# Second layer norm's rows in a buffer of their own, low-rank sums in the ring of back banks, and a new order of work

## What is computed

```python
x = x + tanh(g_xattn[0]) * cross_attention(layernorm(x), ctx)      # q with rotary positions, k and v of 128 context rows, 8 heads
x = x + tanh(g_ffn[0])   * ffn0(layernorm(x))
x = x + tanh(g_xattn[1]) * (layernorm(x) @ W1.T + mean_part(ctx) + b)
x = x + tanh(g_ffn[1])   * ffn1(x_normed)                           # x_normed = layernorm(x)

# ffn0, with ternary weights (values -1, 0, 1 times a scale of the row)
h = x @ Wfc.T + gate * (x @ v.T @ fast_b.T @ u.T)                   # 2048 hidden numbers, rank 16
out = relu(h)**2 @ Wproj.T

# ffn1, with ternary weights and rows rounded to integers of at most 127
h = gelu(rint(127 * n(x) / max|n(x)|) ... @ w1.T + b1)              # n: RMS norm
out = rint(127 * n(h) / max|n(h)|) ... @ w2.T + b2
```

## Time and profile before

| | busy us | share of the span | instructions |
|---|---|---|---|
| PE | 1094.3 | 93% | 8270 |
| DVE | 953.5 | 81% | 1989 |
| ACT | 799.4 | 68% | 1575 |
| POOL | 591.5 | 50% | 567 |

### The profile page before, as it was taken

How to read it: one execution, slowest core, us unless ns; L and a number is a source line. 1 busy time by engine, 2 the same in 40 slices (tenths; PEclk the granted TensorE clock), 3 DMA queues, 4 the chain that set the end, 5 groups by cost and what they waited for, 6 DMA issues and landing times.

```text
span 1176.7 us, 22172 instructions
## 1 busy us (share of the span) xinstructions
PE 1094.3 (93%) x8270; PEld 677.4 (58%) x8558; DVE 953.5 (81%) x1989; ACT 799.4 (68%) x1575; POOL 591.5 (50%) x567
## 2 busy tenths in 40 slices
PE   5776699999999999999899999999999999999997
PEld 5544456474655656475655656475656656564654
DVE  4796868778789888788878798898879886998667
ACT  3988947676683958576584857676674957586545
POOL 4243545464653746454544656555545555564431
PEclk9888799999999999999999999999999999999999
DMA  9959651434525343533625252443436242432210
GB/s 339 367 153 309 204 122 47 99 81 77 126 59 117 69 116 73 104 81 68 126 53 136 57 123 68 89 110 77 108 55 145 45 119 61 103 69 55 68 45 27
DMA packets 273802, 128.11 MB, mean 109 GB/s; under 512 B 247568, under 2 KB 248080, under 8 KB 272016
## 3 DMA queue, kind: packets, MB, share of 16 engines
q1 hardware_dynamic: 273136, 125.73, 41.8%
q10 hardware_dynamic: 560, 0.96, 0.3%
HBM read 57.19 MB, written 8.39 MB: 56 GB/s over the span
## 4 chain that ended last, share of the span: by engine, by line
PE 55%; ACT 17%; DVE 16%; POOL 5%; issue 4%; DMA 2%; SPq 0%; ACTq 0%; DVEq 0%
PE ps L1861 14%; PE ps L1835 10%; PE ps L1904 6%; PE ps L1920 5%; PE ps L1788 5%; ACT e L966 4%; PE ps L1735 4%; PE ps L1883 4%; ACT rl L1002 3%; ACT hid L1007 2%; ACT sq L1013 2%; PE ps L1760 1%; DVE st L1369 1%; PE ps L1841 1%; PE ps L1775 1%
## 5 line engine op out<-in xcount | busy, mean ns | idle before, releaser
L1835 PE MATMUL ps<-xT,fcT 128*128 128x256 f16 x2048 | 262.5, 276 | 10.8 <-ACT rl L1002 7.1
L749 POOL TENSOR_TENSOR rs<-ve,nhalf 128x1 f32<-128x1 f32 x160 | 101.7, 638 | 306.1 <-DVE ve L1374 222.8
L1861 PE MATMUL ps<-pjT,hid 128*128 128x512 fp8e4 x1024 | 232.3, 379 | 2.6 <-POOL hid L776 1.6
L1835 PEld LDWEIGHTS ps<-xT,fcT 128*128 128x128 fp8e4 x2048 | 200.1, 99 | 52.6 <-ACT rl L1002 10.0
L776 POOL TENSOR_TENSOR hid<-sq,hid 128x512 f16<-128x512 f32 x128 | 163.1, 1279 | 80.3 <-ACT sq L1013 79.4
L1861 PEld LDWEIGHTS ps<-pjT,hid 128*128 128x128 f16 x1024 | 98.0, 98 | 98.3
L1002 ACT ACTIVATE rl<-ps,rsf 128x256 f32<-128x256 f32 x256 | 106.4, 469 | 25.0 <-PE ps L1841 24.8
L966 ACT ACTIVATE e<-ps,nmb,sig 128x128 f32<-128x128 f32 x256 | 113.1, 462 | 7.2 <-DVE nmb L1412 6.9
L1904 PE MATMUL ps<-w1T,q4T 128*128 128x512 fp8e4 x480 | 114.2, 379 | 0.7 <-issue 0.6
L1058 ACT ACTIVATE q<-h 128x2048 f16<-128x2048 f32 x30 | 57.3, 1910 | 79.3 <-DVE h L1531 79.3
L781 POOL TENSOR_TENSOR e<-e,einv 128x512 f32<-128x512 f32 x64 | 70.1, 1100 | 78.5 <-DVE einv L1416 78.5
(11 more groups left out here) (243 smaller groups left out, 2025.7 us busy)
## 6 DMA issues: line engine op xcount, KB each, us to landing
xb<-in_x SPq DMA_DIRECT2D x16, 512.0 KB, 3.6
xa<-in_x SPq DMA_DIRECT2D x15, 512.0 KB, 4.0
out<-r SPq DMA_DIRECT2D x30, 256.0 KB, 2.3
rope<-in_rope SPq DMA_DIRECT2D x16, 384.0 KB, 3.2
h<-in_w1T SPq DMA_DIRECT2D x6, 1024.0 KB, 5.8
h<-in_w2T SPq DMA_DIRECT2D x6, 1024.0 KB, 6.4
h<-in_wkvT SPq DMA_DIRECT2D x2, 1024.0 KB, 12.6
hid<-in_w_fc SPq DMA_DIRECT2D x2, 1024.0 KB, 9.9
```

Source lines behind the costliest of these rows:

```text
L1835: pe.matmul(ps[:, FFN0 + m % 2, a * G:(a + 1) * G], fcT[:, k, f * P:(f + 1) * P], xT2[:, xs, k, :], start=(xs == 0 and k == 0), stop=False)
L1861: mm = pe.matmul(ps[:, FFN0 + t, :], hid[:, xs, c, t * P:(t + 1) * P], pjT[:, c, :], start=(c == 0 and xs == 0), stop=(c == FC - 1 and xs ...
```

## The change

1. `xn2` gets its own buffer of 128 x 2 x 512 numbers. `ln2_apply(g)` now waits for `x2lo` of group g-1, its own earlier reader. To make room, constants and small rows of the prologue (`ones`, `small`, `wsum`, `fold1`, `bnd`, `gsf`, `bxbc`, `tb2`) share buffers with things that are used later or earlier.
2. The low-rank rows and sums of group g go, from group 2 on, to the ring of back banks: the ring has 14 slots for a group, and slot 11 of group g-2 is theirs, columns 0 to 255 for the rows, 256 to 511 for the sum. w2's slots move by one. `low_rows(g)` waits for `h_done` of group g-2 in place of group g-1's down product. `up` of m=1 waits for the down product of g-1, and the scores of g > 2 wait for `low_r(g-1)`. The first w1 piece of the last group but one waits for the low-rank remainder of the last.
3. The softmax takes banks 2 and 3 together: three maxima and three scalings for each group in place of four and four.
4. The MAGIC subtraction for ffn1's input rows moves from DVE (L1509, 30 instructions) to ACT, as a copy with a bias in a function `q4_integers`, with a semaphore `q4_int`; `ln3_apply` waits for it of group g-1.
5. All number tables are new. Up to about 105 us the order of every engine's work is as before.

In all PE has the same number of instructions, DVE 62 fewer, ACT 30 more, POOL and SP as many as before.

```diff
-        xn2 = rl
+        xn2 = sb("xn2", [P, TILES, D], F32)
...
+        def s_pair():
+            return slice(ROW_TILES[2], ROW_TILES[3] + 1)
...
-            return ps[:, BACK0 + (13 * g + slot) % 3, :]
+            return ps[:, BACK0 + (14 * g + slot) % 3, :]
+
+        def low_bank(g):
+            return ps[:, FFN0 + 1, :] if g < 2 else back_bank(g - 2, 11)
...
             PE=dict(
-                low_sum=((34,), (62,), (97,), (134,), (175,), (214,), (253,), (291,), (332,), (371,), (411,),
+                low_sum=((34,), (62,), (99,), (136,), (177,), (215,), (253,), (291,), (332,), (372,), (411,),
...
-                need(sp, q4_done, 2 * TILES, g, 2 * t + 1)
+                need(sp, q4_int, TILES, g, t)
...
-                act.activation(lowsum[:, :], ps[:, FFN0 + 1, 0:G], ACT.Copy).then_inc(part_b, 1)
+                act.activation(lowsum[:, :], low_bank(g)[:, 0:G], ACT.Copy).then_inc(part_b, 1)
...
-                act.activation(tlow[:, :], ps[:, FFN0 + 1, 0:G], ACT.Copy).then_inc(low_b, 1)
+                act.activation(tlow[:, :], low_bank(g)[:, G:2 * G], ACT.Copy).then_inc(low_b, 1)
...
+            def q4_integers(g, t):
+                if final(g):
+                    act.wait_ge(turned_q4, t + 1)
+                    dst, src = q4T_of(g)[:, :, t * P:(t + 1) * P], chunks_of(FFN0 + t)
+                else:
+                    need(act, q4_done, TILES, g, t)
+                    dst, src = q4[:, t, :], x3n[:, t, :]
+                act.activation(dst, src, ACT.Copy, bias=-MAGIC).then_inc(q4_int, 1)
...
             def soft_max(g, n):
-                need(dve, s_ps, 4, g, n)
-                scores = s_bank(g, n).rearrange("p (h s) -> p h s", h=4)
-                dve.tensor_reduce(nmx[:, n, :], scores, axis=AX.X, op=ALU.max, negate=True).then_inc(s_max, 1)
+                units = slice(2, 4) if n == 2 else slice(n, n + 1)
+                need(dve, s_ps, 4, g, units.stop - 1)
+                if n == 2:
+                    scores = ps[:, s_pair(), :].rearrange("p b (h s) -> p b h s", h=4)
+                else:
+                    scores = s_bank(g, n).rearrange("p (h s) -> p h s", h=4).unsqueeze(1)
+                dve.tensor_reduce(nmx[:, units, :], scores, axis=AX.X, op=ALU.max, negate=True).then_inc(s_max, 1)
...
-                need(dve, s_max, 4, g, n)
-                dve.tensor_scalar(nmb[:, n, :], nmx[:, n, :], sig[:, :], None, ALU.mult).then_inc(s_bias, 1)
+                need(dve, s_max, 3, g, n)
+                dve.tensor_scalar(nmb[:, units, :], nmx[:, units, :], sig[:, :], None, ALU.mult)\
+                    .then_inc(s_bias, units.stop - units.start)
...
             def ln2_apply(g, t):
-                if t == 0:
-                    need(dve, sq_done, FC // 2, g - 1, FC // 2 - 1)
+                need(dve, x2lo, TILES, g - 1, t)
...
             def ln3_apply(g, t):
+                need(dve, q4_int, TILES, g - 1, t)
...
-                if final(g):
-                    return
-                need(dve, q4_done, 2 * TILES, g, 2 * t)
-                dve.tensor_scalar(q4[:, t, :], z, MAGIC, None, ALU.subtract).then_inc(q4_done, 1)
...
-                else:
-                    need(pe, h_done, 4 * TILES, g - 3, 4 * TILES - 1)
+                elif g > 2:
+                    need(pe, low_r, 2, g - 1, 0)
...
-                need(pe, down_mul, TILES, g - 1, 1)
+                if g < 2:
+                    need(pe, down_mul, TILES, g - 1, 1)
+                else:
+                    need(pe, h_done, 4 * TILES, g - 2, 5)
...
                 elif m == 1:
-                    need(pe, low_r, 2, g, 0)
+                    need(pe, down_mul, TILES, g - 1, 1)
+                    if g < 2:
+                        need(pe, low_r, 2, g, 0)
...
-                need(pe, h_done, 4 * TILES, g, t + 5)
+                need(pe, h_done, 4 * TILES, g, t + 6)
```

More of the change, by code:

```diff
@@ L116, in build @@
         q5 = sb("q5", [P, HID], F16)
+        bxbc = q5[:, 0:2 * D].bitcast(F32)
         hT = sb("hT", [P, TILES, FC, P], F16)
@@ L152, in build @@
         tg = sb("tg", [P, 4], F32)
-        small = sb("small", [P, SMALL], F32)
+        small = sq[:, 0, 0:SMALL]
+        wsum = sq[:, 0, 144:152]
+        fold1 = sq[:, 0, 128:144]
+        bnd = sq[:, 0, 112:128]
+        gsf = sq[:, 0, 96:112]
         sig = sb("sig", [P, 1], F32)
@@ L556, in build @@
-            ACT=dict(q4_end=(548, 549), wq=(3,), k_hi=(17,), v_hi=(19, 20), tanh=(1,), wo=(18,),
-                     evac=(6, 14, 15, 29, 33, 35, 36, 37), rows=(4, 7, 10, 21), whole=(5, 8, 12, 28), low=(32,),
-                     wx=(46,), sums=(39, 40, 41, 42, 43, 44, 45, 47), lift=(54, 61, 62, 67, 71, 76, 79, 80)),
+                     thr=(9, 15, 20, 37, 45, 47, 48, 51), wo_max=(12,), v_top=(22,), wo_scale=(26,), wo_lo=(30,),
+                     mix_row=(42,), low_rank=(41,), v_parts=(28,), wx_max=(52,), hidden=(53,), wx_scale=(57,),
@@ L559, in build @@
+                     wx_lo=(75,), row_scale=(55,), mean=(69,), diag=(54,), round=(71, 77, 79, 85, 88, 91, 96, 98),
+                     clip=(78, 84, 86, 87, 92, 93, 99, 108)),
+            ACT=dict(wq=(3,), k_hi=(17,), v_hi=(19, 20), tanh=(1,), wo=(18,), evac=(6, 14, 15, 29, 33, 35, 36, 37),
+                     rows=(4, 7, 10, 21), whole=(5, 8, 12, 28), low=(32,), wx=(51,),
+                     sums=(39, 40, 41, 42, 43, 45, 46, 47), lift=(54, 61, 64, 66, 73, 74, 79, 80)),
             POOL=dict(whole=(18, 19, 20, 21), rot_k=(5, 6), csb=(4,), low_zero=(13,)),
@@ L1081, in run @@
                         x3_hi(g, t)
+                    for t, g in due("ACT", "q4", p):
+                        q4_integers(g, t)
                     for t, g in due("ACT", "gelu", p):
@@ L1715, in prepare @@
                     pe.wait_ge(c_scd, 1)
-                    pe.matmul(ps[:, 0, :], ones[:, :], diag, start=True, stop=True).then_inc(c_scps, 1)
+                    pe.matmul(ps[:, 0, :], ones, diag, start=True, stop=True).then_inc(c_scps, 1)
                 for _ in here("PE", "mean", p):
@@ L1720, in prepare @@
                     pe.wait_ge(c_mx, 4)
-                    pe.matmul(ps[:, 7, 0:8], ones[:, :], wsum[:, :], start=True, stop=True).then_inc(c_asumps, 1)
+                    pe.matmul(ps[:, 7, 0:8], ones, wsum, start=True, stop=True).then_inc(c_asumps, 1)
             def q_proj(g, hg):
@@ L1895, in w1_up @@
                     need(pe, x3_done, TILES, g, u - ring + 2)
-                elif not final(g) and not final(g + 1):
-                    need(pe, s_exp, 4, g + 2, 1)
+                elif not final(g):
+                    if final(g + 1):
+                        need(pe, low_r, 2, g + 1, 0)
+                    else:
+                        need(pe, s_exp, 4, g + 2, 1)
                 if n == 0 and final(g):
-                    pe.wait_ge(end_q4, t + 1)
+                    need(pe, q4_int, TILES, g, t)
                 elif n == 0:
```

343 lines of the change are left out of this document (169 added, 174 removed), and 123 rows, old and new, of tables (down, exp, h, hid).

## The result

Over seven runs each the changed kernel takes 1185.74 us (1183.75 to 1188.91) and the kernel before 1177.32 (1174.56 to 1180.03). The ratio is 1.0077, with a 95% interval of 1.0062 to 1.0092: slower by 8 us, where 1172 and a gain were forecast. The profiled execution took 1183.75, its span is 1181.6.

A forecast was written before the change was run, and what follows sets the result against it. PE's list was taken as the bound, so only its waits (28.1 us idle in 960) could be won. Terms -2.0 - 3.9 - 3.4 - 2.8 - 1.6 + 6.3 = -7.4 took 1178.8 to 1171.4; forecast 1172, range 1160 to 1186.

The forecast's parts named there:

- item 7: DVE loses 33 us of work, ACT gains 18.8; both run beside PE, priced at nothing outside items 2 and 6.
- Item 1: End of weight preparation: two down pieces before the last up piece fill most of PE's 2.69 us ReLU wait; -2.0 us.
- Items 2 and 5: Longer covers cut PE's waits: scores 5.9 to 2.0 us (-3.9), output projection 2.6 to 1.0 (-1.6).
- Item 3: Granted-clock dips behind two 2.0 us waits, at group 2's low-rank rows and the scores, go: -3.4 us.
- Item 4: Low-rank waits fall from 6.3 to 3.5 us, -2.8; sign: no wait over 0.7 at low-rank rows but in group 7.
- Item 6: New PE waits at first w1 piece, group 0's mix, w1's second tile (transposed integers) and tail: +6.3 us, bounds 0 and +13.
- C: Rival: integers queue on ACT, so transposes and w1's second tile come late; about +7, 1187 us; chance 0.13.
- D: Rival: more is won, items 2 to 5 at their good ends; -18, to 1162 us; chance 0.08.
- B: Rival: nothing moves, since removed waits make PE reach the next chain sooner and new ones arise; 1178 us; chance 0.29.
- The rule on shared ports: DVE and POOL lock shared ports, waiting passes to DVE's next instruction: DVE wins 14.7 of 24.5 us; item 2 some 0.5 smaller.

The follow-up runs named there:

- v13: Kernel before plus 30 idle ACT copies of 128x512 to 16 bits that wait for nothing, integers still on DVE: 1.0069 of the kernel before.
- v12: Kernel before with only the MAGIC subtraction moved to ACT, placed where DVE's rounding ended in the earlier trace: 1.0141 of the kernel before.
- v3: Changed kernel, new order, with the 30 MAGIC subtractions back on DVE right behind the rounding: 1.0151 of the kernel before.
- v16: v6 with, in groups 2, 7, 9 and 12, the ReLU that down waits for put ahead of exponentials or integers on ACT: 1.0046 of the kernel before.
- v6: Changed kernel with its large SBUF tiles moved up by 64 bytes, so transposed tiles start at 256 modulo 512: 1.0024 of the kernel before.
- after_again: The changed kernel, unchanged, run again on the same chip in the same hours as the kernel before: 1.0081 of it.
- before_again: The kernel before, unchanged, run again for its trace beside the others; one execution took 1173.04 us.
- v10: Kernel before, its order and tile addresses kept, with only the low-rank rows and sum moved into the ring of 14 slots: 1.0022 of the kernel before.

## Why the prediction was wrong

**What bounds the kernel.** PE's list was taken as the only bound, and item 7 priced ACT's 19 us of added work "at nothing outside of items 2 and 6". This is the step that failed. ACT's work for one pair of halves in the kernel before, two ReLUs and two squares (start, us, instruction), and what follows:

```profile
657.39 0.84 ACT L1002 ACTIVATE rl<-ps,rsf 128x256 f32<-128x256 f32 x2
658.26 0.63 ACT L1007 ACTIVATE hid<-rl 128x512 f16<-128x512 f32 x1
658.80 0.61 ACT L1013 ACTIVATE sq<-rl 128x512 f32<-128x512 f32 x1
659.32 0.44 ACT L966 ACTIVATE e<-ps,nmb,sig 128x128 f32<-128x128 f32 x1
```

From start to start the pair takes ACT 1.93 us (durations overlap and can't be added), and PE computes a pair in 1.96 (657.19 to 659.15, low-rank parts included). Behind it stand four exponentials, another 1.73 us. An average of 68% hides a stage in which ACT is as full as PE. All of ACT's idle time before its ReLUs was 25.0 us for 128 pairs; it is 21.9 in v13 and 19.0 in v12. Against the nothing of item 7, v13 measures 0.69% or 8 us for the time alone, and v12 1.41% or 17 us with the waiting. Both stand in the old order. In the new one the price of ACT's work is not shown by itself: v3, which gives the work back to DVE, is slower, and v16 only moves waits about.

The forecast was 7.4 us less. At good addresses the changed kernel takes 2.8 us more (v6), so some 10 us of the miss lie in the sum's terms, below, and the rest in the start of the tiles, for which it had no term.

**Item 1, leaving the weight preparation.** Forecast -2.0. The changed kernel is 0.8 ahead at the low-rank rows of group 1, by the comparison of places above, which tells nothing here, since two executions of the kernel before differ by 4.6 at that place. The waits below tell more. By the low-rank rows of group 3 the lead was to be 5.7, with the wait of 2.0 and its clock dip; it is 0.3, and waits of 1.02, 0.94, 1.51, 0.88, 1.14 and 0.86 us have come in between 183 and 304 us. PE at the end of the preparation in the changed kernel (start, us, instruction, idle before):

```profile
133.52 1.05 PE L1859 MATMUL ps<-xT,fcT 128*128 128x256 f16 x8 [1.60 <-ACT rl L1005]
...
137.31 1.05 PE L1859 MATMUL ps<-xT,fcT 128*128 128x256 f16 x8 [1.66 <-ACT rl L1005]
...
140.25 1.05 PE L1859 MATMUL ps<-xT,fcT 128*128 128x256 f16 x8 [0.80 <-ACT rl L1005]
...
144.12 3.63 PE L1885 MATMUL ps<-pjT,hid 128*128 128x512 fp8e4 x16 [1.73 <-issue]
```

The wait of 2.69 is now one of 1.60, 1.66 and 0.80 before three up pieces, and the down pieces put in to fill it wait 1.73 themselves, where the prediction allowed under 1. `after_again` shows 1.60, 1.66, 0.81 and 1.73, and `before_again` the 2.69: nothing was won at this place.

**Items 2 and 5.** The scores' waits went from 5.9 to 5.3 and not to 2.0; `before_again` has 5.4, so this is no change. The longest fell from 2.0 to 0.9, as the longer covers promised, but there are nine in place of seven: a mean cover says nothing on how many fall short. This is the largest term of the sum that didn't come, 3.9 forecast and 0.6 at most measured. The output projection's waits are below what the view lists, better than the 1.0 forecast.

**Item 3, the clock.** The outcome is right: no window of 5 us from 160 to 1120 us is under 1.00. The kernel before has two such dips, the second (0.91 and 0.75, behind 580 us) as the prediction assumed it from the wait alone. The reason given, that the waits of 2.0 us go and the dips with them, doesn't hold as a rule: waits of that length came back, and the clock stayed at 1.00 in the windows of 5 us around them, in the changed kernel (2.15 at 831 us) and in v3 (2.87 at 739), while v16 has 0.66 behind one of 2.25. The prediction's "+1.7 if a new wait of that length arises" was spared by luck. The mean granted clock of the profiled executions went from 0.978 to 0.988; over all seven of the changed kernel it is 0.984 to 0.988, and `before_again` has 0.983.

**Item 4, low-rank product.** Right in size: 2.6 us (1.6 and 1.0) where 3.5 was forecast and 6.3 stood, though its sign was not met, since the longest wait at the low-rank rows, 0.86, stands at group 3 and not at 7. The ring by itself earns nothing (v10), as said.

**Item 6, new waits.** Forecast +6.3, bound 13. The new or grown waits in the list above are 3.4 at the query projection, 4.6 less POOL's 1.6 at down, 3.0 at w2, 4.0 at w1 and 1.7 at the mix: some 15, over the bound (against them, up's waits for ReLUs fell from 2.9 to 1.0). This is the term of the sum that was mis-sized. Part of it is the landing times, taken as fixed from the rows before while the diff moved the sources' start. That is 0.5 to 0.6% by v6, 6 to 7 us, and no term or rival of the prediction had it.

**Item 7.** Sixteen merged maxima save 0.16 us each, where 0.15 was estimated; DVE's busy time fell from 953.5 to 920.1, the 33 us forecast. That it would be hidden was right for the joined softmax. Where DVE lost the subtractions, the price lay on ACT.

**Rivals.** C gave 1187 and is nearest in time, but by luck, and not by its place: w1's waits for transposed integers are 1.1 us, not 10. Its mechanism, integers that queue on ACT, is real, in front of ReLUs. In the new order the integers stay the better choice (v3), so what C charged to the integers is mostly paid back by the tables. D had nothing for it. B, at good addresses, comes close: 1.0024, with PE's waits moved about rather than removed.

**The rule on shared ports.** By it only 14.7 of the 24.5 us of subtractions would be won, the rest going over to DVE's next instruction. The runs speak against that much being passed on. DVE is busy for 932.2 us in v12 and for 950.8 to 953.5 in eight executions with the subtractions: 18.6 to 21.3 less. In the new order it is 918.5 in `after_again` and 944.7 in v3, 26.2 more for subtractions of 27.2.

The account, in ratios: parts in the old order at good addresses 1.0161 (of it the integers 1.0141, the ring 1.0022, the softmax -0.0007), new tables -0.0137, start of the tiles +0.0053 to +0.0057, in all 1.0077 to 1.0081. What stays open is the split of v12's second half, what ACT's added work costs within the new order, and whether an order made anew for the kernel without part 4 would beat the kernel before.

## What to carry to other kernels

When a diff adds, drops or merges buffers, work out where the sources of its transposes start: an edit of 64 bytes cost half a per cent here, and its mark is a higher DMA share at equal GB/s. Before work moves to an engine that is idle on average, take the piece of the loop in which it feeds the bounding engine, and compare what both need for it, from start to start; here 30 instructions of 0.62 us cost 8 us, though the average left a third of the time free. A change that comes with a new order is judged with a third kernel that has its parts in the old order at the same addresses, since the order can hide what a part costs.

## What the hardware showed that was not expected

- A DMA transpose reads more slowly from a source that doesn't start at a multiple of 256 bytes: 2.7 to 3.1 us for 512 columns of x in two parts, 3.7 to 4.3 for the hidden rows; starts at 192, 320 and 384 modulo 512 are alike. For 512 columns of integers in one part it is 2.3 to 2.4. The start of the destination makes no difference (2.7 and 2.8 with it at 320).
- ACT is busy for 68% of the span, and 30 added copies of 0.62 us that wait for nothing still lengthen the kernel by 8 us, 0.69% [0.42, 0.96] (v13).
- Durations on ACT overlap: a ReLU pair, two squares, then the next instruction start 0.87, 0.54 and 0.52 us apart and are listed with 0.84, 0.63 and 0.61.
- A wait of PE doesn't set the granted clock by its length alone: it fell to 0.66 in the 5 us behind one of 2.25 (v16) and stayed at 1.00 around one of 2.87 (v3).
- One maximum over 1024 numbers of each partition in two banks takes 1213 ns, two over 512 take 1372; one scaling of 8 columns 271 ns, one of 4 columns 435 in the same profile; why the smaller one takes longer no run shows.
